# Softmax denominators of a gated cross-attention kernel: the fourth step's exponentials go into the ones-matmul as they are

## The reference

```python
lat, ctx = layer_norm(_layernorm(x)), layer_norm(context)
q = lat @ Wq;  k, v = split(ctx @ Wkv);  k = apply_rope(k, cos, sin)
attn = clip(einsum('bhnd,bhsd->bhns', q, k) * DHEAD ** -0.5, -11.0, 11.0)
attn = softmax(attn, axis=-1)              # numerator and denominator
x = x + tanh(g_xattn) * (einsum('bhns,bhsd->bhnd', attn, v) @ Wo + bo)
x = x + tanh(g_ffn) * ffn(_layernorm(x))   # router over 4 experts, 2 for each row
```

## Time and profile before

| | us |
|---|---|
| median of three timed runs | 1186.5 |
| lowest and highest | 1182.81 and 1187.26 |
| the profiled execution: its own time | 1181.76 |
| the profiled execution: span of the core | 1180.0 |
| TensorE busy | 1118.4 |
| VectorE busy | 1015.7 |
| ScalarE busy | 649.8 |
| GpSimd busy | 609.8 |
| attention part | about 45 to 872 |
| expert part | about 872 to 1180 |

### The profile page before, as it was taken

How to read it: one execution, slowest core, us unless ns; L and a number is a source line. 1 busy time by engine, 2 the same in 40 slices (tenths; PEclk the granted TensorE clock), 3 DMA queues, 4 the chain that set the end, 5 groups by cost and what they waited for, 6 DMA issues and landing times.

```text
span 1180.0 us, 22084 instructions
## 1 busy us (share of the span) xinstructions
PE 1118.4 (95%) x8087; PEld 752.5 (64%) x8087; DVE 1015.7 (86%) x1751; ACT 649.8 (55%) x1223; POOL 609.8 (52%) x593
## 2 busy tenths in 40 slices
PE   5799999999999999999999999998789999999997
PEld 3455555555556565555555556664359999999886
DVE  6699999898999989999999998879697887875686
ACT  4554557655556665545575554544456677674331
POOL 5334466343346534334653434217747878887650
PEclk9999999999999999999999999999989999999998
DMA  6100100000000000000000004001454556665212
GB/s 170 41 10 10 36 24 15 10 10 11 16 30 24 15 10 10 10 28 19 23 15 10 11 18 144 10 10 41 151 185 157 201 188 219 218 211 193 70 37 72
DMA packets 67114, 79.18 MB, mean 67 GB/s; under 512 B 10936, under 2 KB 60480, under 8 KB 67008
## 3 DMA queue, kind: packets, MB, share of 16 engines
q1 hardware_dynamic: 64688, 71.47, 19.0%
q0 software_dynamic: 2304, 6.29, 1.6%
q10 hardware_dynamic: 16, 0.00, 0.0%
HBM read 64.65 MB, written 13.11 MB: 66 GB/s over the span
## 4 chain that ended last, share of the span: by engine, by line
PE 68%; DVE 16%; POOL 6%; issue 5%; ACT 2%; DMA 1%; another core or an unknown queue 1%; SPq 1%; DVEq 0%; POOLq 0%; ACTq 0%
PE pv L1543 14%; PE sc L1529 12%; PE kv L1474 5%; PE kv L1476 4%; PE kv L1475 4%; PE sc L1474 4%; DVE acc L1020 4%; PE sc L1476 4%; PE sc L1475 4%; PE tr L1515 3%; PE mi L1474 3%; PE mi L1475 2%; PE mi L1476 2%; POOL slots_x L642 2%; PE mi L1553 2%
## 5 line engine op out<-in xcount | busy, mean ns | idle before, releaser
L801 ACT ACTIVATE prob<-sc 128x1024 f32<-128x1024 f32 x256 | 249.3, 1028 | 214.5 <-PE sc L1529 206.0
L613 POOL TENSOR_TENSOR rot_s<-k_raw,sinb 128x256 f32<-128x256 f32 x128 | 107.4, 839 | 385.0 <-ACT k_raw L749 384.9
L1543 PE MATMUL pv<-prob,val 128*32 128x512 f32 x2048 | 247.1, 600 | 2.1 <-DVE recip L1039 2.1
L1529 PE MATMUL sc<-q_hid,big 64*128 64x512 f32 x1536 | 214.4, 411 | 6.3 <-ACT prob L801 6.3
L1005 DVE TENSOR_SCALAR prob<-prob 128x1024 f32<-128x1024 f32 x256 | 184.2, 735 | 37.7 <-ACT prob L801 35.2
L1529 PEld LDWEIGHTS sc<-q_hid,big 64*128 64x128 f32 x1536 | 135.0, 185 | 111.4 <-issue 65.8
L1020 DVE TENSOR_TENSOR acc<-acc,prob 128x1024 f32<-128x1024 f32 x128 | 196.6, 1557 | 0.0
L617 POOL TENSOR_TENSOR rot_c<-rot_c,rot_s 128x256 f32<-128x256 f32 x128 | 115.2, 900 | 44.5 <-DVE rot_c L994 29.8
L1543 PEld LDWEIGHTS pv<-prob,val 128*32 128x32 f32 x2048 | 56.8, 110 | 112.5 <-issue 91.8
L1474 PE MATMUL kv<-big,acts 128*128 128x512 f32 x256 | 114.1, 446 | 6.3 <-DVE rot_c L994 5.0
L662 POOL TENSOR_TENSOR big<-val,big 128x512 fp32r<-128x512 f32 x72 | 93.0, 1299 | 28.4 <-ACT big L828 24.3
(11 more groups left out here) (250 smaller groups left out, 2508.8 us busy)
## 6 DMA issues: line engine op xcount, KB each, us to landing
val<-in_L_ffn_w SPq DMA_DIRECT2D x18, 1024.0 KB
prob<-in_L_ffn_w SPq DMA_DIRECT2D x18, 1024.0 KB, 8.0
rows<-in_ctx SPq DMA_DIRECT2D x32, 128.0 KB, 2.2
w_raw<-in_L_xattn_Wq SPq DMA_DIRECT2D x16, 256.0 KB, 2.8
w_raw<-in_L_xattn_Wo SPq DMA_DIRECT2D x64, 64.0 KB
slots_x<-c_aff SPq DMA_DIRECT2D x1, 3840.0 KB, 13.5
rows<-slots_x SPq DMA_DIRECT2D x15, 256.0 KB, 8.0
slots_y<-acc SPq DMA_DIRECT2D x15, 256.0 KB, 2.2
```

The source lines that it names most:

```text
L613: g.tensor_tensor(rot_s[:].rearrange("p (h a c) -> p h a c", h=4, a=2), kh[:, :, ::-1, :], sinb[:, t].unsqueeze(1).to_broadcast([P, 4, 2, ...
L801: a.activation(prob[:, s % 2, i, :], sc[i][:], ACT.Exp, scale=DH ** -0.5).then_inc(exp_done[i], 1)
L1529: last = mm(sc[i][:, h * N:(h + 1) * N], kst[rows_h, u % 2, j, lk, t * P:(t + 1) * P], q_sp[rows_h, p % 2, lq, :], start=lk + lq == 0, sto ...
L1543: last = mm(pv[g * 32:(g + 1) * 32, :], val[:, u % 2, 2 * c + i, at:at + 32], prob[:, s % 2, i, h * N:(h + 1) * N], start=c == 0 and i == ...
```

## The change

The running sum stops at the third step (c = 2). At c = 3 nothing is added. The denominators are made from two sources: the sum of three steps in `acc`, and the fourth step's clamped exponentials, which are in slot 1 of `prob`. Both are multiplied with ones into the same accumulation in `mi`, so there are 16 matmuls for a pair in place of 8, and four adds of 128x1024 in place of six. `summed[i]` counts two for a pair instead of three, and the waits on it are renumbered: ScalarE waits for the same adds as before at c = 0, 2 and 3, and at c = 1 for the third step's add of the pair before (the last one there is). `denominators` waits for the third step's add, and before its second half for the fourth step's clamp.

```diff
@@ exps (ScalarE)
-                wait(act, summed[i], q * 3 + (-1, 0, 1, 1)[c])
+                wait(act, summed[i], q * 2 + (0, 0, 1, 1)[c])
@@ sums (VectorE)
-                if c == 0:
+                if c in (0, CH - 1):
                     return
@@
-                    dve.wait_ge(summed[i], q * 3 + c - 1)
+                    dve.wait_ge(summed[i], q * 2 + c - 1)
@@ denominators (TensorE)
                 for i in range(2):
-                    pe.wait_ge(summed[i], (pair_no(b, p) + 1) * 3)
+                    pe.wait_ge(summed[i], (pair_no(b, p) + 1) * 2)
                     for g in range(4):
                         half, h = g // 2, g % 2
                         at = h * N + half * QH
-                        last = mm(mi[g * 32:(g + 1) * 32, 0:QH], ones[:, 0:32], acc[:, i, at:at + QH],
-                                  start=i == 0, stop=i == 1)
+                        mm(mi[g * 32:(g + 1) * 32, 0:QH], ones[:, 0:32], acc[:, i, at:at + QH], start=i == 0, stop=False)
+                for i in range(2):
+                    pe.wait_ge(clamped[i], (pair_no(b, p) + 1) * CH)
+                    for g in range(4):
+                        half, h = g // 2, g % 2
+                        at = h * N + half * QH
+                        last = mm(mi[g * 32:(g + 1) * 32, 0:QH], ones[:, 0:32], prob[:, 1, i, at:at + QH],
+                                  start=False, stop=i == 1)
                 last.then_inc(den_ready, 1)
```

## The result

Six runs of each on one chip: 1195.7 us (1191.8 to 1198.4) after, 1185.8 us (1182.8 to 1187.4) before. The ratio is 1.0083, with a 95% interval of 1.0059 to 1.0106: slower by 0.8%, 7 to 13 us. Two executions of the later runs, one of before at 2154 us and one of `last_four` at 1310 us, were in a slower state of the chip and are left out of every figure here. The profiled execution has a span of 1191.9 us, 11.9 more than that of before.

What follows compares the result with a forecast made beforehand. TensorE's instruction stream was taken to bound attention: +24.4 - 2.25 - 2.64 - 3.7 - 2.3 - 1.0 = +12.5 us, 1194.3 on the profiled execution, 1199.0 on the median, given as 1198.0; range 1193 to 1203, 8 of 10 within 1190 to 1207.

Steps and rivals of the forecast that it cites:

- 28 blocks at 0.87: Added denominator blocks on TensorE ahead of step (3,2,4) each cost 0.87 us: +24.4 us.
- (a): Denominator waits for the fourth add at (1,1,0), (2,1,0), (3,1,0) go, 0.75 us each: -2.25 us.
- (b): VectorE's backlog in two-step stretches from 96.17 and 187.76, the latter also one batch later, all goes: -2.64 us.
- (c): Key-transpose stalls on GpSimd at (0,2,1), (1,2,1), (2,2,1) go, through added matmuls and a shorter subtraction: -3.7 us.
- (d): Stretch set by GpSimd's 24 scatters: they start 2.3 us earlier, and a shorter subtraction gives -1.0 us.
- The three blocks in this stretch taken at nothing: Added blocks at (3,2,4), (3,3,0), (3,3,4) cost nothing beside GpSimd's scatters and the expert-weights wait; 2.6 us without that cover.
- (e): End of attention: the last block needs no add but has four halves of 0.43 us; nothing won, nothing lost.
- Rival 1: Only direct stalls go; backlog, longer subtraction and scatters' start have other causes: +19.5, 1206.0 us; chance 0.17.
- rival 2: The chain of waits is right and VectorE paces the kernel: -1.4, 1185.1 us; chance 0.08.
- rival 4: New matmuls slip into gaps of TensorE's stream and cost nothing: -11.9, 1174.6 us; chance 0.02.
- Rival 3: GpSimd relief goes further, all scatters running at their shortest: 7 us more at most, 1191 us; chance 0.06.
- stream theory: In attention TensorE's own instructions set the pace; a block costs 0.87 us at 28 places.

Runs made afterwards that it cites:

- last_four: The change in pairs 28 to 31 alone, the other pairs as before: ratio 0.9983 (0.9958 to 1.0008), medians 1182.2 against 1185.6 us before.
- adds_only: The changed kernel without the added fourth-step ones-matmuls, so the denominators miss that step: ratio 0.9893, medians 1173.0 against 1184.8 us before.
- adds_idle: The change plus two 128x512 adds nobody else waits for per removed add, except in the last pair: ratio 1.0144, 1202.1 against 1184.8 us before.
- mm_only: The kernel before plus the eight extra ones-matmuls per pair, all three adds kept: ratio 1.0175, medians 1204.0 against 1184.8 us before.
- mixed: Seven pairs as in the change, eight with both tiles folded into one sum, 17 as before: ratio 0.9988, medians 1182.1 against 1185.1 us before.
- seven_pairs: The change in pairs 3, 11, 19 and 28 to 31 only, the other 25 as before: ratio 0.9952, medians 1178.4 against 1184.8 us before.
- other_pairs: The change in all pairs except 3, 11, 19 and 28 to 31, which stay as before: ratio 1.0162, medians 1203.1 against 1185.6 us before.
- fold_all: Against before, both tiles of every step added into one sum: 7 adds, 4 ones-matmuls per pair; ratio 1.0143, medians 1201.2 against 1185.1 us.

## Why the prediction was right

**The view chosen to tell the pace.** Starts of equal steps, not busy shares and not the chain. This carried the result: step lengths in every experiment are those of before plus or minus a whole or half block (6.93, 5.63) where nothing stalls. The chain's 4% for line 1020 was the trap it was called: removing half of those adds gave 12 us, where the earlier trace rows would have promised 23.

**28 blocks at 0.87.** Right, 0.865 each, +24.2.

**(a)** Right, -2.25 forecast and -2.24 measured. The steps are 6.93 where an undisturbed one is 6.93.

**(b)** Forecast -2.64; the places that it named gave -1.7, and a place that it did not name 0.3 more. The 0.9 at (0,1,1) and (0,1,2) went. Of the two pairs of steps like the earlier trace rows only the second step of each, (0,3,0) and (1,3,0), gave something back, 0.4 us each: (0,2,7) and (1,2,7) are as long as before in the change, in `adds_only` and in `adds_idle`. The fourth step's adds are not what makes them long: in before those of (0,2,7) begin at 194.21, when that step is over; in `last_four`, which has no edit before the last batch, (0,2,7) is 0.58 us shorter by itself, so this excess is not stable from one trace to the next. A further 0.28 at (0,2,4) went that I had not counted. The step that failed is "I take all of it as gone": two steps were priced as one, though the fourth step's adds stand ahead of the second only.

**(c)** Forecast -3.7, measured -3.9. `adds_only` and `mm_only` show that both halves of the argument were at work and that either of them alone was worth as much as I gave it, or more. GpSimd's part was under-priced, 1.97 us of its queue and not 0.97: the rows showed the row scales behind the subtraction, and I did not ask whether the adds held them too. It changed nothing, since the stall was only 1.30 long.

**(d)** The scatters' start: forecast -2.3, measured -2.3. From the first scatter to the end of the last: forecast -1.0 (the subtraction), measured -1.7, the subtraction and the rotation's sum before it, which I had not priced. The three blocks in this stretch taken at nothing: right, (3,2,4) pays 0.87 and (3,2,5) gives it back and more, since its wait for GpSimd, 3.1 us, is gone. The first expert matmul keeps its distance to the end of the last scatter, 24.7 and 24.9 us, ScalarE being held 8.5 us for the weights as it was 8.3.

**(e)** Right: nothing won or lost. The last blocks and the first expert matmul of after, against the earlier trace rows:

```profile
881.97 1.05 PE L1553 MATMUL mi<-acc,ones 128*32 128x256 f32 x16
882.84 1.05 PE L1559 MATMUL mi<-prob,ones 128*32 128x256 f32 x16
883.81 0.39 PE L1474 MATMUL sc<-acts,big 128*128 128x256 f32 x1
```

1.84 us from the first to the expert part, 1.83 before.

**The sum.** +12.5 forecast for the part in attention, +10.7 measured, of which -1.5 is the clock at (3,2,2), which the change did not touch: the mechanisms give +12.2. That this is within 0.3 of the forecast is in part luck: (b) gave 0.6 less than its term and (d) 0.7 more. On the medians the forecast of 1198.0 stood against 1195.7, inside the narrower 1193 to 1203 too; as a difference, 9.9 us, where 11.5 had been forecast. Of the signs that were named, the denominators have no wait left on line 1020 and none on the clamps, and the first scatter stands at 812.27 for 812.5. That last hit holds 1.0 us of loads ahead of the first score and -1.5 of the clock, neither of them forecast. The expert part starts 11.75 us later, with the same two in it. Rival 1 falls with (c) and (d), rival 2 with `adds_only`, rival 4 with `mm_only`. Rival 3 had nothing in the scatters it was drawn from: 1.27 us on average before, 1.28 after.

## What to carry to other kernels

When two engines are both near full, take equal steps and compare the starts of their first instruction: the engine whose stream alone explains the shortest step sets the pace, and an instruction added to it costs its own length everywhere but where a stall already stands. Work taken from the other engine is worth only the excess of stalled steps over their undisturbed twins, and it can be had by making the exchange at those places alone: the same edit lost 10 us in all 32 pairs and won 6 in seven of them.

An engine's free share is no budget. VectorE had 6 to 8% free on average between 200 and 700 us, and one more add for each pair made the kernel 16 us slower, although it took half a block off TensorE; the waits say that it came ahead of what TensorE waits for next.

## What the runs showed of the hardware

**The granted clock after the same idle.** At step (3,2,2) TensorE stands 1.94 us waiting for the low part of the queries (line 1000). The stretch of that step in before, in the change, and in `last_four` (span, busy time of PE, PEld, DVE, ACT and POOL, then TensorE's granted clock, DMA share, GB/s):

```profile
772.60:785.90 13.30, 11.36 (x78) 8.29 (x74) 10.22 (x24) 3.12 (x6) 1.45 (x2) 0.87 0.01 1
```

```profile
789.60:801.50 11.90, 9.96 (x80) 7.21 (x76) 10.26 (x24) 3.12 (x6) 1.45 (x2) 1.00 0.00 0
```

```profile
772.90:786.60 13.70, 11.76 (x78) 8.01 (x74) 10.22 (x24) 3.12 (x6) 1.45 (x2) 0.85 0.01 1
```

TensorE's idle time is 1.94 us in all three, and VectorE, ScalarE and GpSimd are as busy in one as in another. Yet the clock fell to its lower level, half speed, for 3.4 us in before and `adds_idle` just as TensorE took up work again, for 3.4 us about the start of the next step in `adds_only` and `mixed`, twice with 3.4 us between in `last_four`, and not at all in these two steps of the change, `mm_only`, `seven_pairs`, `other_pairs` and `fold_all`. A fall costs 1.5 us, the two of `last_four` 3.1. I did not expect it to differ between kernels that are alike at that place, and what decides it stays open; a difference of that size in the last batch can't be put down to an edit.

**GpSimd beside VectorE's two-input adds.** The same subtraction of 128x512: 1.32 us with no add beside it, 1.74 with adds of 128x512, 2.28 with adds of 128x1024. The adds pay as well, but only those that meet it. In before the 64 adds of the third step (c = 2) have a median of 1.21 us and the 64 of the fourth (c = 3) one of 1.69; together they make the 1.65 of the earlier trace rows. The change takes the fourth step's away, and the third step's are as they were, 90.4 us in sum before and 90.5 after:

```profile
L1020 DVE TENSOR_TENSOR acc<-acc,prob x64: 1204/1213/1756, 62.5 to 877.3; 128x1024 f32<-128x1024 f32 x64
```

**One scatter of 4.7 us.** In `adds_only`, `adds_idle`, `other_pairs` and `last_four` one of the eight scatters that read `rows`, the fifth or the sixth, took 4.69 or 4.70 us. In the other six kernels none of the 24 took more than 1.97. Three pairs of kernels make the same adds from pair 28 on and differ in it, and from the first scatter to the end of the last they are 2.6 us apart each time: `last_four` and `seven_pairs` 49.22 and 46.65, `other_pairs` and before 50.95 and 48.38, `adds_only` and the change 49.25 and 46.64. Nothing in the edits goes with it, and what decides it was not tried.

**What is left without the two.** Us in attention against before; the fall of the clock and the slow scatter are those of one execution each.

| kernel | in attention | clock | slow scatter | rest | expected |
|---|---|---|---|---|---|
| the change | +10.7 | -1.5 | | +12.2 | +12.5 |
| `mm_only` | +19.2 | -1.5 | | +20.7 | +21 |
| `adds_only` | -10.4 | 0 | +2.6 | -13.0 | -12 |
| `adds_idle` | +19.8 | 0 | +2.6 | +17.2 | +18 |
| `seven_pairs` | -7.0 | -1.5 | | -5.5 | -5 |
| `other_pairs` | +18.5 | -1.5 | +2.6 | +17.4 | +17.5 |
| `last_four` | -0.3 | +1.6 | +2.6 | -4.5 | -3 to -4 |

The rest of `last_four` has 0.7 us in it from batch 0, where it has no edit. So the stream theory's number is met within about 1 us in all seven. It was missed in `fold_all` and `mixed`, where VectorE was given more to do.
